# A shorter front: half of q and k drained by ScalarE, the scales prepared by GpSimd, and loads that wait for landings

## The reference

```python
xn = layernorm(x)
q, k, v = Wq@xn + bq, Wk@ctx + bk, Wv@ctx + bv        # per batch, rows are mixed
p = softmax(qh @ kh.T / 8)                            # per head, 64 x 64
x = x + Wo @ (p @ vh) + bo
w = (w_int - zeros[group]) * scales[group]            # gate, up: 512 x 1792; down: 1792 x 512
xn2 = layernorm(x)
x = x + (silu(xn2 @ w_gate) * (xn2 @ w_up)) @ w_down
```

## Time and profile before

| | us |
|---|---|
| median of the runs | 435.28 (433.78 to 435.38) |
| the profiled execution | 434.65 |
| its span | 432.7 |
| busy: TensorE, VectorE, ScalarE, GpSimd | 411.5, 325.7, 320.7, 252.7 |

### The profile page before, as it was taken

How to read it: one execution, slowest core, us unless ns; L and a number is a source line. 1 busy time by engine, 2 the same in 40 slices (tenths; PEclk the granted TensorE clock), 3 DMA queues, 4 the chain that set the end, 5 groups by cost and what they waited for, 6 DMA issues and landing times.

```text
span 432.7 us, 10699 instructions
## 1 busy us (share of the span) xinstructions
PE 411.5 (95%) x4228; PEld 320.3 (74%) x4228; DVE 325.7 (75%) x578; ACT 320.7 (74%) x529; POOL 252.7 (58%) x266
## 2 busy tenths in 40 slices
PE   7978989998999899999999999999999999999994
PEld 4756667786877677777777878677877888888872
DVE  4668857889887778788887777787887667667676
ACT  2326798785877688687778888687888998988970
POOL 3433478698666654665473954755566555555561
PEclk9999999999999999999999999999999999999999
DMA  6899799995920000002011001000000000001003
GB/s 215 228 192 312 182 298 306 273 245 108 274 84 24 2 5 23 26 2 75 16 37 26 2 0 27 26 2 26 26 26 2 2 1 8 18 24 51 1 0 97
DMA packets 27287, 35.55 MB, mean 82 GB/s; under 512 B 2366, under 2 KB 18918, under 8 KB 27238
## 3 DMA queue, kind: packets, MB, share of 16 engines
q1 hardware_dynamic: 19282, 27.43, 19.4%
q0 software_dynamic: 7456, 7.34, 10.9%
q10 hardware_dynamic: 500, 0.11, 0.1%
HBM read 30.62 MB, written 4.25 MB: 81 GB/s over the span
## 4 chain that ended last, share of the span: by engine, by line
PE 78%; DVE 10%; issue 4%; ACT 3%; POOL 1%; DMA 1%; SPq 1%; POOLq 0%; DVEq 0%; ACTq 0%
PE banks L742 22%; PE banks L744 20%; PE banks L755 11%; PE banks L756 10%; PE banks L640 4%; DVE yT L1016 3%; PE banks L680 2%; PE banks L669 2%; PE banks L658 2%; PE banks L650 2%; ACT banks L536 2%; DVE st L903 2%; DVE t_sb L1001 1%; PE banks L699 1%; DMA xn<-in_L_ffn_down_s 1%
## 5 line engine op out<-in xcount | busy, mean ns | idle before, releaser
L536 ACT ACTIVATE banks<-banks,ratio 128x512 f32<-128x512 f32 x336 | 207.8, 661 | 42.4 <-PE banks L744 32.6
L1016 DVE SCALAR_TENSOR_TENSOR yT<-banks,sd,yT 128x512 f32<-128x512 f32 x208 | 154.4, 748 | 51.8 <-PE banks L756 51.1
L742 PE MATMUL banks<-xT,wgu 128*128 128x512 f32 x448 | 181.9, 406 | 4.6 <-DVE t_sb L1001 4.6
L744 PE MATMUL banks<-xT,wgu 128*128 128x512 f32 x448 | 175.3, 391 | 0.0
L399 POOL TENSOR_TENSOR t_sb<-t_sb,u_sb 128x512 f32<-128x512 f32 x56 | 74.1, 1324 | 62.2 <-DVE t_sb L1001 62.0
L742 PEld LDWEIGHTS banks<-xT,wgu 128*128 128x128 f32 x448 | 84.1, 188 | 25.6 <-issue 6.0
L744 PEld LDWEIGHTS banks<-xT,wgu 128*128 128x128 f32 x448 | 84.4, 188 | 15.3
L755 PE MATMUL banks<-hr,wd 128*128 128x512 f32 x224 | 89.4, 399 | 2.6 <-POOL hr L412 1.6
L756 PE MATMUL banks<-hr,wd 128*128 128x512 f32 x224 | 87.6, 391 | 0.0
L412 POOL TENSOR_TENSOR hr<-t_sb,hr 128x512 fp32r<-128x512 f32 x56 | 72.6, 1297 | 5.1 <-ACT hr L558 0.7
L755 PEld LDWEIGHTS banks<-hr,wd 128*128 128x128 f32 x224 | 42.0, 188 | 17.5 <-DVE yT L1016 8.2
(11 more groups left out here) (91 smaller groups left out, 372.0 us busy)
## 6 DMA issues: line engine op xcount, KB each, us to landing
wgu<-z_out SPq DMA_DIRECT2D x14, 512.0 KB, 8.3
x_sb<-in_x SPq DMA_DIRECT2D x16, 256.0 KB, 5.7
out<-x_sb SPq DMA_DIRECT2D x16, 256.0 KB, 2.1
wgu<-in_L_ffn_gate_w POOLq DMA_DIRECT2D x7, 512.0 KB, 7.3
wgu<-in_L_ffn_up_w POOLq DMA_DIRECT2D x7, 512.0 KB, 10.9
wd_in<-in_L_ffn_down_w SPq DMA_DIRECT2D x7, 512.0 KB, 7.7
yT<-in_L_ffn_down_z SPq DMA_DIRECT2D x7, 512.0 KB, 6.9
ctx_sb<-in_ctx SPq DMA_DIRECT2D x12, 256.0 KB, 3.8
```

What stands on the lines that cost most here:

```text
L536: act.activation(banks[:, bank, :], banks[:, bank, :], ACT.Copy, scale=ratio[:, m, g, it:it + 1]).then_inc(done[n % 2], 1)
L742: pe.matmul(banks[:, bank, :], w, xT[:, c % 2, 0, g, :], start=g == 0, stop=False, skip_group_check=True)
L744: pe.matmul(banks[:, bank, :], w, xT[:, c % 2, 1, g, :], start=False, stop=True, skip_group_check=True).then_inc(full[n % 2], 1)
L1016: dve.scalar_tensor_tensor(y, bank, sd[:, it, b:b + 1], y, ALU.mult, ALU.add).then_inc(s_free, 1)
```

## The change

1. **q and k.** For tiles 0 to 4 project(t) starts bank b = 1 with a matmul that puts the biases there: two rows, high and low part, against two rows of ones (ones_r, b_two). The projection is added on top, and ScalarE takes the bank by a plain copy. VectorE still takes bank b = 0 with the bias added. From tile 5 on all is as before. GpSimd makes the two rows in two_rows().
2. **Scales.** prepare() is now ten operations on GpSimd that add twice the floor to scales below it; only the reciprocal, of three of the four groups, stays on VectorE (inverse). ratios() waits for it.
3. **Orders.** The lists of all engines in the front are new: on TensorE the scales' transposes stand behind project(1), project(3) ahead of values(1), and the filler counts are others; on VectorE less_max(1) stands ahead of residual(0); on GpSimd the additions of pieces 1 to 3 stand behind weigh(1), weigh(2) and the last power, and ratios() stands ahead of weigh(3).
4. **Loads.** SP waits for the landing of piece k before later ones: zeros 2 behind piece 0, zeros 3 behind piece 1, the down weights behind piece 2, zeros 5 behind piece 3.

```diff
@@ SP
-            for k in range(4):
-                load_zeros(k)
+            load_zeros(0)
+            load_zeros(1)
             load_x(4)
+            sync.wait_ge(s_wgu[0], 16)
+            load_zeros(2)
             load_ctx(4)
             sync.wait_ge(s_wgu[1], 16)
+            load_zeros(3)
             load_x(5)
+            sync.wait_ge(s_wgu[2], 16)
             load_down(0)
-            sync.wait_ge(s_wgu[2], 16)
             load_ctx(5)
             load_zeros(4)
+            sync.wait_ge(s_wgu[3], 16)
             load_zeros(5)
             load_x(6)
-            sync.wait_ge(s_wgu[3], 16)
             load_zeros(6)
@@ GpSimd
+            def two_rows():
+                b = b_row[:, 0:2, :]
+                hi, two = (a.rearrange("a (m o) -> a m o", m=2) for a in (b_hi, b_two))
+                pool.wait_ge(s_bias, 32)
+                pool.tensor_copy(hi, b).then_inc(s_two, 1)
+                pool.wait_ge(s_two, 2)
+                pool.tensor_tensor(two, b, hi.bitcast(F32), ALU.subtract).then_inc(s_two, 1)
+                pool.wait_ge(s_two, 3)
+                pool.tensor_copy(two[0:1], hi[0:1].bitcast(F32)).then_inc(s_two, 1)
+            def prepare():
+                pool.wait_ge(s_scl, 2)
+                pool.tensor_scalar(flat(ab), flat(sg), 0.0, None, ALU.max).then_inc(s_pr, 1)
+                pool.tensor_scalar(flat(sp_), flat(sg), 0.0, None, ALU.min).then_inc(s_pr, 1)
...
+                pool.tensor_tensor(flat(sp_), flat(sg), flat(ab), ALU.add).then_inc(s_pr, 1)
-            for t in range(PRE):
+            rstd(0, 0)
+            two_rows()
+            for t in range(1, PRE):
                 rstd(0, t)
+            weigh(0)
             add_weights(0)
-            weigh(0)
-            add_weights(1)
-            raised()
-            add_weights(2)
+            prepare()
             weigh(1)
             rstd(1, 0)
-            add_weights(3)
+            add_weights(1)
             weigh(2)
             rstd(1, 1)
+            add_weights(2)
+            ratios()
             weigh(3)
+            rstd(0, 4)
             rstd(1, 2)
-            rstd(0, 4)
             rstd(1, 3)
-            ratios()
+            add_weights(3)
@@ ScalarE
+            def take_qk(t):
+                act.wait_ge(s_bQK, t + 1)
+                if t >= 1:
+                    act.wait_ge(s_bS, t)
+                act.copy(qkT[:, 1, :], banks[:, pair("QK", t) + 1, :]).then_inc(s_qka, 1)
@@ TensorE
+                if t <= PRE:
+                    two = b_two.rearrange("a (m o) -> a m o", m=2).unsqueeze(2).to_broadcast([2, 2, NC, D])
+                    pe.matmul(banks[:, at + 1, :].rearrange("p (m c o) -> p m c o", m=2, c=NC), ones_r, two,
+                              start=True, stop=False, skip_group_check=True)
...
-            stir(1)
+            stir(3)
             pe.wait_ge(s_wT, 1)
             project(0)
@@ VectorE
+            def inverse():
+                dve.wait_ge(s_pr, 10)
+                dve.reciprocal(ab[:, :, 1:NG, :], sp_[:, :, 1:NG, :]).then_inc(s_inv, 1)
...
+            less_max(1)
+            take_qk(2, 0)
             dve.wait_ge(s_wT, 3)
             residual(0)
-            less_max(1)
-            take_qk(2, 0)
-            take_qk(2, 1)
             invert(1)
...
+            invert(3)
+            inverse()
```

More of the change, by code:

```diff
@@ L155, in xattn_ffn @@
         s_raw = xn2[:, 1, 0:2 * P].rearrange("r (a p) -> r a p", a=2)
-        b_row = xn2[0:1, 1, 2 * P:2 * P + 4 * D].rearrange("a (m o) -> a m o", m=4)
-        ones = xn2[0:1, 0, 2 * P:3 * P]
+        b_row = xn2[0:2, 1, 2 * P:2 * P + 4 * D].rearrange("a (m o) -> a m o", m=4)
+        b_hi, b_two, ones_r = (xT[0:2, 1, 0, 0, i * P:(i + 1) * P] for i in range(3))
+        ones = xn2[0:2, 0, 2 * P:3 * P]
         qkT = sb("qkT", [P, 2, 2 * NC * D])
@@ L474, in _ @@
             for m, v in enumerate((bq, bk)):
[L475 removed]
+                load(s_bias, b_row[:, m, :], v.partition_broadcast(2))
             load(s_wsm2, wraw[:, 2, :], Wv)
@@ L567, in _ @@
             act.copy(sd[:, :, :].rearrange("p g c -> p (g c)"), banks[:, 4, ng:ng + NI * NC]).then_inc(s_scl, 1)
-            norm1(2)
-            power_of(0)
+            take_qk(1)
+            norm1(3)
             act.wait_ge(s_wT, 3)
             take_v(0)
-            norm1(3)
+            take_qk(2)
             take_a(0)
@@ L577, in _ @@
             take_a(1)
+            take_qk(3)
             power_of(2)
+            norm2(0)
             take_v(2)
-            norm2(0)
+            take_x(0)
+            take_a(2)
             power_of(3)
-            take_a(2)
-            take_x(0)
             norm2(1)
@@ L601, in _ @@
                 act.copy(xT[:, 0, 0, g, t * P:(t + 1) * P], blocks(RING_BANK + h)[:, g, :]).then_inc(done, 1)
+                if h == 0:
+                    take_qk(PRE)
             act.wait_ge(s_prep, 1)
@@ L786, in _ @@
             pe.wait_ge(s_bias, 32)
-            pe.matmul(banks[:, 7, 0:2 * D], ones, b_row[:, 0:2, :], start=True, stop=True).then_inc(s_brow, 1)
-            stir(1)
+            pe.matmul(banks[:, 7, 0:2 * D], ones[0:1, :], b_row[0:1, 0:2, :], start=True, stop=True).then_inc(s_brow, 1)
+            stir(3)
             pe.wait_ge(s_wT, 1)
             project(0)
[L791 to L797, removed]
+            pe.wait_ge(s_bqk, 1)
             pe.wait_ge(s_wsm2, 32)
@@ L808, in _ @@
             stir(2)
-            pe.wait_ge(s_qk, 4)
-            project(2)
+            score(0)
+            project(1)
+            pe.wait_ge(s_sc, 48)
+            ng, nd = 2 * NG * NI, NI * NC
+            pe.transpose(banks[:, 4, 0:ng], s_raw[0:ng, 0, :], ident[0:ng, 0:ng])
+            pe.transpose(banks[:, 4, ng:ng + nd], s_raw[0:nd, 1, :], ident[0:nd, 0:nd]).then_inc(s_trs, 1)
+            stir(2)
+            stir(1)
             pe.wait_ge(s_wT, 3)
             values(0)
-            stir(1)
             pe.wait_ge(s_sub, 1)
             score(1)
+            wait_qk(pe, 1)
+            project(2)
+            stir(1)
             pe.wait_ge(s_v, 1)
@@ L819, in _ @@
             apply(0)
-            stir(2)
+            wait_qk(pe, 2)
+            project(3)
             pe.wait_ge(s_x1, 1)
             values(1)
-            stir(1)
-            pe.wait_ge(s_qk, 6)
-            project(3)
             pe.wait_ge(s_sub, 2)
             score(2)
-            stir(2)
+            stir(1)
             pe.wait_ge(s_v, 2)
@@ L840, in _ @@
             mix(2)
-            pe.wait_ge(s_scl, 2)
-            turn_x(0)
-            stir(1)
+            stir(2)
             apply(2)
-            stir(2)
+            stir(3)
             pe.wait_ge(s_x1, 3)
@@ L853, in _ @@
             apply(3)
-            stir(3)
+            stir(4)
             turn_x(2)
@@ L1069, in _ @@
             less_max(2)
-            take_qk(3, 1)
+            shift(1, 0)
             residual(1)
@@ L1073, in _ @@
             most(3)
-            shift(1, 0)
+            stats(1, 1)
             less_max(3)
-            stats(1, 1)
-            invert(3)
+            rest_x(0)
             shift(1, 1)
             residual(2)
-            rest_x(0)
+            invert(3)
+            inverse()
+            stats(0, 4)
             stats(1, 2)
-            stats(0, 4)
             rest_x(1)
+            shift(0, 4)
             shift(1, 2)
             residual(3)
-            shift(0, 4)
             stats(1, 3)
-            divide()
             shift(1, 3)
@@ L1098, in _ @@
                                   ALU.subtract).then_inc((s_lastlo, s_free)[h], 1)
-            take_qk(4, 1)
             for q in range(PLACES):
```

85 lines of the change are left out of this document (45 added, 40 removed).

## The result

The changed kernel takes 439.94 us (median of 4 executions, 439.91 to 441.41), the kernel before 435.33 in the same job. The ratio is 1.012, 95% interval 1.0101 to 1.0139: the change is slower by 1.2%, outside the range of 431.2 to 437.0. Yet in the profiled execution the front got shorter, by more than forecast, and the loop behind it lost more than twice that.

A forecast was written before the change was run, and what follows sets the result against it. It took a chain of waits around the engines, once per front tile, to set the first gate/up matmul. Front terms summing to -1.6 us take the profiled 434.65 to 433.05, or 433.7 on the median's footing; range 431.2 to 437.0.

The forecast's parts named there:

- The step that failed: Loads: later additions and zeros cost nothing, as steps 0 and 1 need only pieces 0 and 1.
- the sum: All front terms together: first gate/up matmul 1.2 to 1.9 us earlier, 1.6 taken; loads counted at nothing.
- The rival of the late weights: In the loop, piece 5 lands late and stalls step 4 by 3.3 us: 437.0, or 439 with step 6; chance 0.16.
- residual(0): Front up to tile 0's residual: it starts at 25.0 us instead of 24.77, +0.2 taken, bounds 0 and +1.3.
- residual(0) to mix(1): Front, tile 1: less_max(1) ahead and takes no longer between put mix(1) at 27.8 to 28.5, -3.4 to -2.7 us.
- mix(1) to mix(2): Front, next tile: same links in both kernels, 5.01 us, so mix(2) at 32.8 to 33.5.
- mix(2) to mix(3): Front, last tile: reciprocal and ratios() ahead of weigh(3) make it 6.45 us, 1.85 longer.
- mix(3) to the start: End of the front up to the first gate/up matmul: two VectorE links go, 7.5 us instead of 7.82.
- prepare(): GpSimd's ten operations on the scales: 4.5 us, from about 18.8 to 23.3, hidden in its wait for invert(1).
- that rival (0.18): Slow small operations on GpSimd or VectorE delay weigh(1) by 0.7 us and the two-row bias by 1.0: 435.3; chance 0.18.
- the case without a rival: Whole kernel by the sum alone, with bounds of bias rows and stall: said to span 432.9 to 434.9 us.
- The clock rival: In the front, added filler raises TensorE's clock before 23 us: 432.7 if at 19, 431.5 if at 15; chance 0.21.

The follow-up runs named there:

- e6: The kernel before with the change's loads alone: SP's order and waits, additions of pieces 0 to 3 at the change's places; 440.25 us, ratio 1.0112.
- e12: The changed kernel with zeros 4, zeros 5, x(6) and the additions of pieces 1 to 3 issued earlier, ratios() left ahead of weigh(3); 433.08 us, ratio 0.9953.
- e7: The changed kernel with SP's loads as before and the additions of pieces 1 to 3 brought forward on GpSimd; 435.02 us, ratio 0.9989.
- e10: The kernel before, old orders and work, with the loads and places of the additions of e12; 434.81 us, ratio 0.9987.
- e8: As e7, with ratios() moved behind the third power of the second norm; 433.29 us, ratio 0.9971.
- e2: The changed kernel with zeros 5 and x(6) issued ahead of SP's wait for piece 3's landing; 437.58 us.
- e4: The changed kernel with only zeros 5 issued ahead of SP's wait for piece 3, x(6) behind it; 440.95 us, one execution.
- e9: As e12, but with ratios() moved behind the third power of the second norm; 432.74 us, ratio 0.9959.

## Why the prediction was wrong

**The step that failed** is the one on the loads: "I cost this at nothing in the sum, because steps 0 and 1 need only pieces 0 and 1". It looked at the piece that a step needs and not at the queues: what piece 3's landing holds back in SP's list (zeros 5, x(6)), and what stands behind those two in GpSimd's and VectorE's lists. It cost 9.4 us in the loop, where the sum had 0. e6 shows it alone. The rest of the sum, 1.6 us off the front, was borne out in one variant and not in another, both with the change's orders except for the additions and with nothing lost in the loop: e12, with thin loads, is 1.9 us below the kernel before in its job, and e7, with the old loads, 0.0.

**The rival of the late weights** had the right place and the right kind, at 0.16. Its terms were off. It said that it decides when piece 3 lands after about 52 us, and that piece 3 should be there by 50. Piece 3 was issued at 42.08, earlier than the 44 forecast, took 9.2 us where 6 were allowed, and landed at 51.24. Step 4 started at 76.18; the sign of this rival was later than 71. It took zeros 5 to be quick, being first in SP's order: they needed 6.9 us. The addition of piece 4 and the loads behind them were in flight at the same time; that this is why was not tested. It priced piece 5's own landing; what bound was one link earlier, GpSimd standing still for zeros 5 and VectorE for x(6), and x(6) in VectorE's list was not in it. It left out zeros 4 behind the down weights (2.3 us relative to the start by the last group of step 0), and the fall of the clock in the waits (2.1 us more between places 8 and 10). It gave 437.0 to 439; 439.94 was measured.

**The front, step by step.** residual(0) was forecast at 25.0 and came at 21.40 in the profiled execution, as the clock rose at 5.3 us instead of 23, which is luck and not the change's (a stall of 2.34 us in it notwithstanding). GpSimd's three operations for the two rows took 1.15 us (1.0 to 1.4 forecast), and project(0) started at 7.24. *residual(0) to mix(1)*: 2.8 to 3.5 forecast, 4.51 measured, with project(3), values(1) and score(2) on TensorE as the longer way and part of it at the lower clock; in e12, where the clock rose at 20.6, mix(1) is at 27.37, where 27.8 was forecast. *mix(1) to mix(2)*: 5.01 forecast, 5.14 measured. *mix(2) to mix(3)*: 6.45 forecast, 6.41 measured, and the profile names weigh(3) as what mix(3) waited 1.56 us for. *mix(3) to the start*: 7.5 forecast, 7.08 measured. *prepare()*: 4.5 us forecast; from 17.99 to 23.29 it took 5.3, the first two operations 1.06 and 1.03 us beside the writing of descriptors, the others 0.24 to 0.60. weigh(1) started right behind it, 0.3 us after invert(1) was done. So that rival (0.18) was half right in its mechanism, but it cost at most 0.3 us on GpSimd and nothing at mix(1), which stood behind TensorE's own work.

Two reckonings of the prediction are slightly off. The first: with its own terms the case without a rival spans 433.2 to 435.2, and not 432.9 to 434.9. Nor does its "below 4.5 us" for prepare() at twice VectorE's price come out: with VectorE's 0.28 us for a two-operand 128x112 operation in the kernel before, seven such and three smaller operations are about 5 us (an estimate). Nothing else hangs on either.

**The clock rival** (0.21) came true in the profiled execution, at 5.3 us, for a reason other than the added filler: the level rises and falls at different instants in executions of one kernel. The Trainium skill (TensorE: Matmul & The Clock Gate, Part 1) warns that the point of the rise varies from run to run, and gives half a microsecond for it; here the two profiles of the kernel before show 14.1 against 23.1 us, and the measurement decides. The early rise didn't bring the result below the kernel before. The four executions of the change lie within 1.5 us although their mean clocks differ (0.976 to 0.992); how much of an early front late loads take back was not measured by itself.

**Where the front's gain came from** is settled in part. In medians, the old front takes 435.05 us with the old loads (the kernel before) and 434.81 with thinner loads that come early enough for the loop (e10); the new front takes 435.02 (e7) and 433.08 (e12). So by this table neither the new orders and moved work nor the thinner transfers gave anything by themselves, and together they gave 1.9 us. Against it stands e8, with the old loads and ratios late, at 433.29. The wait for zeros 3 is part of e10's time, the stalls and the clock are part of every one, and how much each of them made stays open.

## What to carry to other kernels

When a load is made to wait for another's landing, follow the queue it stands in and then every list in which something waits for it: the price here was set by the first instructions behind it, not by the step that reads the data. Work in a front that ends earlier brings its deadlines forward with it, so transfers that are thinned there must be brought forward too. And a single profiled execution of a kernel with short waits carries some us of clock luck in its front; compare the parts behind it, or medians of ten.

## What the runs showed of the hardware

TensorE's level changes several times within a front of 45 us, and differently each time: up at 14.1, down at 24.4, up at 31.2 in one execution of the kernel before, up once at 23.1 in another. It stayed up through the loop, to its last microseconds, in every kernel whose loads were in time, and stood at the lower level for 3.4 to 10.2 us in all in the first 60 us of every loop with late loads. That is by one profiled execution of each kernel.

TensorE stood still in the middle of a burst with no wait that the profile names, always between 18 and 31 us. Those of 0.29 us or more are 1.35, 3.23, 0.94, 2.18 and 3.18 us in the five profiles with SP's old loads. Of the nine with waiting loads five had none, and the others 0.33 (e2), 0.69 (e4), 1.36 in two pieces (e9) and 2.63 in two pieces (the change). So it is more frequent with dense transfers, but dense transfers are not all of it: during the change's stall of 2.34 us the transfers moved only 70 GB/s. In the longest one, 3.23 us, the instruction queue moved a packet (queue q8), but it does so in profiles without a stall too. The cause stays open.
